# Order of TensorE's work in the first edge stage of a two-layer graph network: src transposes ahead of the centring

## The chip, the cores and the metric

One core of one Trainium2 chip. The number that counts is the device time of one execution in microseconds (us), as the median of several runs.

## The reference

`x` has 100,000 rows of 128 float32; `src` and `dst` are 25,000 edges, sorted by `dst`.

```python
# layer 0, on each edge: messages from both ends, maximum over the edges of a destination
x_col = x[col]                       # col = dst, row = src
feat = concatenate([x_col, x[row] - x_col])
messages = relu(feat @ W1 + b1) @ W2 + b2
out0 = segment_max(messages, col)    # 0 for rows without edges
x = layernorm(x + out0)
# layer 1: sum over the edges, two products, a residual product
h = x + segment_sum(x[src], dst)
x = layernorm(x + (relu(h @ W1 + b1) @ W2 + b2) + (x @ Wres + bres))
```

Most rows have no incoming edge. For them both layers are row-wise.

## The kernel before

All rows go through a dense pipeline as if they had no edges, in units of 512 rows (196 units). The rows that are destinations are computed in three edge stages and scattered over the dense result. Edges are cut into 49 groups of 512 (GROUPS), four tiles of 128 each. `walk` writes the order of the work out, and each engine follows it: a head of dense units, a stage that finds places in the table, **the first edge stage** (`step_a`), some dense units, the second edge stage (`step_b`), and dense units to the end. There is no planner; each engine has one fixed order, and semaphores hold it back.

In the first edge stage step s of TensorE works on several groups at once. psE[0] to psE[3] are four banks of PSUM:

- second product of group s-1 (`edge_product2`, L1248), ehT into psE[2];
- first product of group s (`edge_product1`, L1240 and L1242), from the transposed src rows xsT and the transposed dst rows xdT, into psE[0];
- a quarter of a dense unit (h = s mod 4: h=0 the first dense product L1137, h=1 the dense transposes L1118, h=2 and h=3 half of the second dense products L1125 and L1126);
- transposes of the finished rows x1e of group s-2 into psE[1];
- centring of group s-1 (`center_z`, L1257): four pairs of matmuls of zT with a centring matrix into psE[3];
- transposes of the rows gathered for group s+1 (`transpose_in`): the src rows (in edge_rows) into psE[0], then the dst rows (xd_early or src_bc) into psE[1].

All transposes are issued at L1118, in the helper `transpose4`, and show as one line; the operand tells them apart. A float32 matmul shows as two records.

VectorE (`step_a` there) takes per step: a reciprocal of the roots (L738), the scaling of psE[3] into x1e (L748), the running maximum along the edges (L758), the residual that makes zT (L769), statistics of the src rows (L603, L731), the copy of psE[0] into xsT for group s+1 (`copy_xs`, L718), and a dense piece.

ScalarE takes per step:

```python
def step_a(s, n, h):
    scale_xs(s)          # L1036
    relu0(s)             # L1015: psE[0] -> ehT, counts ehT_done
    copy_x1eT(s - 2)     # L1045: psE[1] -> x1eT, counts x1eT_done
    z_var(s - 1)         # L949: squares of psE[3], waits for the centring
    both_roots(s + 1)    # L1025
    copy_xd(s + 1)       # L1004: psE[1] -> xdT, counts xdT_done
    ...                  # then a dense piece by h
```

GpSimd gathers all src rows before this stage's later dst rows, and `gather_dst(g)` waits for the dst transposes of group g-7. SyncE stores x1e, its transpose and the scaled rows of each group; after the stage GpSimd gathers from that table, for which it waits until all of it is stored.

Of the kernel before, what the change touches and what calls it, by code (L numbers as in the profile page):

```python
# [23 lines left out]
def gnn_program(nc, x, src, dst, e_w1, e_b1, e_w2, e_b2, w1, b1, w2, b2, wres, bres, out):  # L24
# [29 lines left out]
    with ctx:  # L54
# [198 lines left out]
        def is_group(g):  # L253
            return 0 <= g < GROUPS

        def src_number(g):
            return TILES * (g + (SLOTS if g >= EARLY else 0))

        def dst_number(g):
            return TILES * (g + (EARLY if g < SLOTS else GROUPS))  # L260
# [7 lines left out]
        def await_landing(eng, n):  # L268

            eng.wait_ge(landed[n % FLIGHT], 16 * (n // FLIGHT + 1))  # L270

        def wait(eng, s, n):

            if n > 0:
                eng.wait_ge(s, n)
# [4 lines left out]
        def cut(t):  # L280
            return slice(t * P, (t + 1) * P)

        def xd_rows(g):

            return (src_bc if g // SLOTS % 2 else xd_early)[:, g % SLOTS, :]

        def group_rows(g):
            return edge_rows[:, g * ROWS:(g + 1) * ROWS]
# [822 lines left out]
        def _(pe):  # L1111
            t_ = nc.tensor

            def transpose4(to, rows, done=None, number=None):
                for t in range(TILES):
                    if number is not None:
                        await_landing(pe, number + t)
                    last = t_.transpose(to[:, cut(t)], rows[:, cut(t)], ident[:, :])  # L1118
                if done is not None:
                    last.then_inc(done, 1)  # L1120
# [12 lines left out]
            def first_product(n):  # L1133
                if is_unit(n):
                    pe.wait_ge(xT_done, n + 1)
                    wait(pe, hT_done, n)
                    t_.matmul(psH[:, :], wc1[:, :], xT[:, n % SLOTS, :], start=True, stop=True).then_inc(w1_done, 1)  # L1137

            def transposed(n):
                if is_unit(n):  # L1140
                    pe.wait_ge(x1_done, n + 1)
                    wait(pe, xT_done, n)
                    transpose4(psT, x1[:, n % 2, :], t_done)
# [7 lines left out]
            def second_half(n, half):  # L1151

                if half == 0:
                    pe.wait_ge(hT_done, n + 1)
                    wait(pe, o_done, n - 1)
                    product_tiles(psY[n % 2], hT[:, n % 2, :], xT[:, n % SLOTS, :], range(TILES // 2))
                else:
                    product_tiles(psY[n % 2], hT[:, n % 2, :], xT[:, n % SLOTS, :],
                                  range(TILES // 2, TILES)).then_inc(y_done, 1)
# [59 lines left out]
                second_product(n - 2)  # L1219
                place(s - 2)  # L1220

            def transpose_in(g):
                if is_group(g):
                    wait(pe, ehT_done, g)
                    transpose4(psE[0], group_rows(g), ts_done, src_number(g))
                    wait(pe, xdT_done, g)
                    wait(pe, x1eT_done, g - 2)
                    transpose4(psE[1], xd_rows(g), tx_done, dst_number(g))

            def lead_a():  # L1230
                pe.wait_ge(match_done, GROUPS)
                pe.wait_ge(places_done, GROUPS)
                transpose_in(0)

            def edge_product1(g):

                if is_group(g):
                    q = g % 2
                    pe.wait_ge(xsT_done, g + 1)
                    t_.matmul(psE[0][:, :], raw[:, W1B, :], xsT[:, q, :], start=True, stop=False)  # L1240
                    pe.wait_ge(xdT_done, g + 1)
                    t_.matmul(psE[0][:, :], wd[:, :], xdT[:, q, :], start=False, stop=True).then_inc(eh_done, 1)  # L1242

            def edge_product2(g):
                if is_group(g):
                    pe.wait_ge(ehT_done, g + 1)
                    wait(pe, max_done, g)
                    t_.matmul(psE[2][:, :], raw[:, EW2, :], ehT[:, g % 2, :], start=True, stop=True).then_inc(m_done, 1)  # L1248

            def center_z(g):  # L1250

                if is_group(g):
                    q = g % 2
                    pe.wait_ge(zT_done, g + 1)
                    wait(pe, x1e_done, g)
                    for t in range(TILES):
                        last = t_.matmul(psE[3][:, cut(t)], zT[:, q, cut(t)], center[:, :], start=t == 0,  # L1257
                                         stop=t == TILES - 1, skip_group_check=True)
                    last.then_inc(bt_done, 1)

            def transpose_x1e(g):
                if is_group(g):
                    pe.wait_ge(x1e_done, g + 1)
                    pe.wait_ge(xdT_done, min(g + 3, GROUPS))
                    wait(pe, x1eT_done, g)
                    transpose4(psE[1], x1e_rows[:, g % 2, :], xt_done)

            def step_a(s, n, h):
                edge_product2(s - 1)
                edge_product1(s)  # L1270
                if n is not None:
                    if h == 0:
                        first_product(n - 1)
                    if h == 1:
                        transposed(n)
                    if h >= 2:
                        second_half(n - 2, h - 2)
                transpose_x1e(s - 2)
                center_z(s - 1)
                transpose_in(s + 1)  # L1280


            def transpose_src(g):
# [41 lines left out]
            t_.matmul(psE[3][:, 0:P], wtmp[:, 1, :], center[:, :], start=True, stop=True)  # L1325
            t_.matmul(psE[3][:, P:2 * P], wtmp[:, 2, :], center[:, :], start=True, stop=True).then_inc(s_pe, 1)
            walk(head, dense, lead_s, step_s, lead_a, step_a, lead_b, step_b)


# [20 lines left out]
```

## Time and profile before

| what | value |
|---|---|
| median of three runs | 1114.36 us (1113.69 to 1115.48) |
| the profiled execution's own time | 1113.68 us |
| its span in the trace | 1111.9 us |
| TensorE busy | 1068.9 us, 96% |
| VectorE busy | 934.9 us, 84% |
| ScalarE busy | 896.9 us, 81% |
| GpSimd busy | 765.8 us, 69% |
| first edge stage | about 264 to 562 us of the span |
| granted TensorE clock, mean | 0.995 |

The busy shares are means over stages with different orders of work. A matmul's record overlaps the next one's, so the distance between starts is what a group of them takes, not the sum of their lengths.

### The profile page before, as it was taken

The page shows a single profiled execution, that of the slowest core. Times are in us where ns is not written, and L with a number is a line of the kernel's source. Part 1 is how long each engine was busy: PE and PEld are TensorE (multiplying, and loading weights), DVE is VectorE, ACT ScalarE, POOL GpSimd, SP SyncE. Part 2 cuts the span into 40 slices and gives each one's busy share as a digit, 9 for nine tenths or more (in the row PEclk, how much of TensorE's full clock was granted, in tenths as well). Part 3 has the DMA queues.
Part 4 walks back from the last instruction along what each step waited for, and adds up shares of the span by engine and source line. Part 5 has one row for each costly group of instructions (what it writes and reads, how often), then busy time and mean ns, then how long its engine had stood idle before and what let it go on. Part 6 is the DMA issues. An engine that isn't in the chain of part 4 may idle for free.

```text
span 1111.9 us, 27074 instructions
## 1 busy us (share of the span) xinstructions
PE 1068.9 (96%) x7463; PEld 835.6 (75%) x7463; DVE 934.9 (84%) x3645; ACT 896.9 (81%) x3888; POOL 765.8 (69%) x798
## 2 busy tenths in 40 slices
PE   5899999999999999999899999999999999999995
PEld 3677877777666666666578888888888878888884
DVE  7799888897888888888868787878787789999993
ACT  2887878787888888888897888888888887777774
POOL 6777777777777777772047777777777777777712
PEclk9999999999999999999999999999999999999998
DMA  5788877875888888877576667676756566666652
GB/s 151 214 244 247 230 244 231 246 233 152 220 222 232 248 232 221 233 223 214 164 232 198 213 191 215 190 214 191 214 166 194 172 202 217 218 217 220 218 171 86
DMA packets 172255, 231.86 MB, mean 209 GB/s; under 512 B 25658, under 2 KB 90791, under 8 KB 172106
## 3 DMA queue, kind: packets, MB, share of 16 engines
q1 hardware_dynamic: 145434, 180.66, 52.0%
q0 software_dynamic: 25088, 48.94, 17.3%
q8 instruction: 62, 1.02, 0.4%
q14 instruction: 87, 0.71, 0.2%
q10 hardware_dynamic: 1584, 0.53, 0.2%
HBM read 129.48 MB, written 102.78 MB: 209 GB/s over the span
## 4 chain that ended last, share of the span: by engine, by line
PE 65%; POOL 19%; issue 8%; DVE 4%; ACT 2%; DMA 1%; SPq 0%; POOLq 0%; DVEq 0%; ACTq 0%
POOL edge_rows L522 17%; PE psY L1125 10%; PE psY L1126 10%; PE psH L1137 10%; PE psE L1118 6%; PE psT L1118 5%; PE psE L1257 4%; PE psE L1126 4%; PE psE L1125 4%; PE psE L1293 4%; PE psE L1248 3%; PE psE L1242 3%; PE psE L1240 3%; POOL xd_early L522 1%; DVE shared L758 1%
## 5 line engine op out<-in xcount | busy, mean ns | idle before, releaser
L1125 PE MATMUL psY<-wc,hT 128*128 128x128 f32 x1568 | 304.1, 276 | 0.5 <-DVE o_rows L646 0.4
L1126 PE MATMUL psY<-wcr,xT 128*128 128x128 f32 x1568 | 303.9, 276 | 0.0
L522 POOL DMA_INDIRECT edge_rows<-x1e_table,idx x196 | 188.8, 963 | 118.5 <-issue 59.4
L526 POOL DMA_INDIRECT out<-edge_rows,idx x196 | 195.0, 995 | 100.0 <-issue 61.9
L1125 PEld LDWEIGHTS psY<-wc,hT 128*128 128x128 f32 x1568 | 240.7, 192 | 13.3 <-issue 13.3
L949 ACT ACTIVATE junk<-psY 128x128 f32<-128x128 f32 x784 | 209.3, 302 | 49.3 <-PE psY L1126 49.1
L1126 PEld LDWEIGHTS psY<-wcr,xT 128*128 128x128 f32 x1568 | 238.8, 193 | 0.0
L522 POOL DMA_INDIRECT edge_rows<-in_x,idx x196 | 189.8, 968 | 65.5 <-issue 59.4
L609 DVE TENSOR_SCALAR x<-x_in,mv,rs 128x128 f32<-128x128 f32 x784 | 221.7, 361 | 0.6
L1137 PE MATMUL psH<-xT,wc 128*128 128x512 f32 x392 | 204.5, 604 | 6.2 <-ACT xT L944 5.5
L1118 PEld LDWEIGHTS psT<-ident,x 128*128 128x128 f32 x784 | 99.2, 143 | 110.1 <-issue 104.1
L949 ACT ACTIVATION_READ_ACCUMULATOR junk<-psY 128x1 f32 x784 | 181.1, 235 | 0.0
L938 ACT ACTIVATE hT<-psH,bias_cols 128x512 f32<-128x512 f32 x196 | 137.5, 701 | 42.1 <-PE psH L1137 42.0
L603 DVE BATCH_NORM_STATS2 bn_a<-x_in 128x6 f32<-128x128 f32 x784 | 164.6, 271 | 4.4 <-DMA x_in<-in_x 4.3
L949 ACT ACTIVATE junk<-psE 128x128 f32<-128x128 f32 x392 | 102.6, 280 | 29.2 <-PE psE L1257 27.9
L1118 PE MATMUL psT<-ident,x 128*128 128x128 f32 x784 | 119.1, 275 | 5.4 <-DVE x L609 5.4
L944 ACT ACTIVATE xT<-psT 128x512 f32<-128x512 f32 x196 | 120.4, 614 | 1.9 <-PE psT L1118 1.9
L522 POOL DMA_INDIRECT xd_early<-in_x,idx x100 | 96.3, 963 | 30.5 <-issue 28.7
L522 POOL DMA_INDIRECT src_bc<-in_x,idx x96 | 93.3, 972 | 29.3 <-issue 27.7
L797 DVE TENSOR_TENSOR_SCAN shared<-mask,shared,psE 128x512 f32<-128x512 bf16 x48 | 61.4, 1280 | 54.1 <-issue 54.1
L646 DVE TENSOR_TENSOR o_rows<-psY,rs 128x512 f32<-128x512 f32 x120 | 83.0, 691 | 6.1 <-DVE rs L629 2.4
L974 ACT ACTIVATE o_rows<-psY,rs 128x128 f32<-128x128 f32 x304 | 87.4, 387 | 0.6 <-DVE rs L629 0.4
(125 smaller groups left out, 1993.4 us busy)
## 6 DMA issues: line engine op xcount, KB each, us to landing
x_in<-in_x SPq DMA_DIRECT2D x196, 256.0 KB
out<-o_rows SPq DMA_DIRECT2D x195, 256.0 KB
src_bc<-src_dram SPq DMA_DIRECT2D x49, 256.0 KB, 4.5
mask<-mask_dram SPq DMA_DIRECT2D x98, 128.0 KB
x1eT_spill<-x1eT SPq DMA_DIRECT2D x49, 256.0 KB, 2.4
x1e_table<-edge_rows SPq DMA_DIRECT2D x49, 256.0 KB, 3.5
x1e_table<-shared SPq DMA_DIRECT2D x49, 256.0 KB, 3.8
x1eT<-x1eT_spill SPq DMA_DIRECT2D x49, 256.0 KB, 3.1
```

Of the source, the lines that this page charges most:

```text
L522: nc.gpsimd.indirect_dma_start(to, None, table, bass.IndirectOffsetOnAxis(idx[:, what, t:t + 1], 0)).then_inc(landed[n % FLIGHT], 16)
L526: nc.gpsimd.indirect_dma_start(table, bass.IndirectOffsetOnAxis(idx[:, SCAT, t:t + 1], 0), frm, None, bounds_check=limit, oob_is_err=False ...
L603: last = v.bn_stats(bn[:, t, :], rows[:, cut(t)])
L609: last = v.tensor_scalar(to[:, cut(t)], rows[:, cut(t)], mv[:, t, 0:1], rs[:, t:t + 1], ALU.subtract, ALU.mult)
L938: a.activation(hT[:, n % 2, :], psH[:, :], ACT.Relu, bias=bias_cols[:, 2:3]).then_inc(hT_done, 1)
L944: a.activation(xT[:, n % SLOTS, :], psT[:, :], ACT.Copy, bias=1.0).then_inc(xT_done, 1)
L949: last = a.activation(unused[:, cut(t)], rows[:, cut(t)], ACT.Square, scale=P ** -0.5, accum_out=var[:, t, 1:2])
L974: last = a.activation(o_rows[:, n % SLOTS, cut(t)], psY[n % 2][:, cut(t)], ACT.Copy, scale=rs[:, slot, TILES + t:TILES + t + 1])
L1118: last = t_.transpose(to[:, cut(t)], rows[:, cut(t)], ident[:, :])
L1125: t_.matmul(to[:, cut(t)], h[:, cut(t)], wc2[:, :], start=t == 0, stop=False, skip_group_check=True)
L1126: last = t_.matmul(to[:, cut(t)], xt[:, cut(t)], wcr[:, :], start=False, stop=t == TILES - 1, skip_group_check=True)
L1137: t_.matmul(psH[:, :], wc1[:, :], xT[:, n % SLOTS, :], start=True, stop=True).then_inc(w1_done, 1)
```

## The change

`transpose_in` is cut in two. The src transposes of group s+1, with their waits for ehT_done and the four landings, come ahead of `center_z(s - 1)`; the dst transposes, with their waits for xdT_done, x1eT_done and their landings, stay behind it. Ahead of the stage both are called for group 0 as before. No other engine's order is touched.

```diff
--- before.py
+++ after.py
@@ -1219,10 +1219,13 @@
                 second_product(n - 2)
                 place(s - 2)
 
-            def transpose_in(g):
+            def transpose_src_in(g):
                 if is_group(g):
                     wait(pe, ehT_done, g)
                     transpose4(psE[0], group_rows(g), ts_done, src_number(g))
+
+            def transpose_dst_in(g):
+                if is_group(g):
                     wait(pe, xdT_done, g)
                     wait(pe, x1eT_done, g - 2)
                     transpose4(psE[1], xd_rows(g), tx_done, dst_number(g))
@@ -1230,7 +1233,8 @@
             def lead_a():
                 pe.wait_ge(match_done, GROUPS)
                 pe.wait_ge(places_done, GROUPS)
-                transpose_in(0)
+                transpose_src_in(0)
+                transpose_dst_in(0)
 
             def edge_product1(g):
 
@@ -1276,8 +1280,9 @@
                     if h >= 2:
                         second_half(n - 2, h - 2)
                 transpose_x1e(s - 2)
+                transpose_src_in(s + 1)
                 center_z(s - 1)
-                transpose_in(s + 1)
+                transpose_dst_in(s + 1)
 
 
             def transpose_src(g):
```

## Rows read from the trace of the kernel before

**Rows 1.** Table by window: PE, PEld, DVE, ACT, POOL busy (instructions), PEclk, DMA share, GB/s.

```profile
450.00:500.00 50.00, 48.46 (x270) 33.92 (x269) 43.66 (x139) 43.36 (x171) 38.10 (x40) 1.00 0.81 227
...
550.00:562.00 12.00, 8.26 (x44) 6.07 (x43) 6.94 (x27) 8.14 (x39) 0.00 (x0) 0.86 0.58 175
```

**Rows 2.** Instructions of the tile psE: count, min/median/max ns, first and last start.

```profile
L1257 PE MATMUL psE<-center,shared x392: 275/275/582, 273.0 to 556.5; 128*128 128x128 f32 x196
```

**Rows 3.** Timeline of TensorE, 413 to 438.5 us and the tail: start, length, [idle before, releaser].

```profile
414.27 1.16 PE L1257 MATMUL psE<-center,shared 128*128 128x128 f32 x8 [0.73 <-DVE shared L769]
415.27 0.60 PE L1118 MATMUL psE<-ident,edge_rows 128*128 128x128 f32 x4
...
417.00 1.02 PE L1240 MATMUL psE<-xsT,raw 128*128 128x512 f32 x2
417.86 1.02 PE L1242 MATMUL psE<-xdT,wd 128*128 128x512 f32 x2
...
419.61 0.60 PE L1118 MATMUL psE<-ident,shared 128*128 128x128 f32 x4
420.05 1.06 PE L1257 MATMUL psE<-center,shared 128*128 128x128 f32 x8
420.94 0.60 PE L1118 MATMUL psE<-ident,edge_rows 128*128 128x128 f32 x4
...
425.28 0.60 PE L1118 MATMUL psE<-ident,shared 128*128 128x128 f32 x4
425.91 1.16 PE L1257 MATMUL psE<-center,shared 128*128 128x128 f32 x8
...
431.65 1.08 PE L1257 MATMUL psE<-center,shared 128*128 128x128 f32 x8
...
436.45 0.60 PE L1118 MATMUL psE<-ident,shared 128*128 128x128 f32 x4
437.80 0.94 PE L1257 MATMUL psE<-center,shared 128*128 128x128 f32 x6 [0.74 <-DVE shared L769]
...
554.80 2.08 PE L1257 MATMUL psE<-center,shared 128*128 128x128 f32 x8 [1.32 <-DVE shared L769]
```

**Rows 4.** Timeline of ScalarE, 413 to 438.5 us.

```profile
415.47 0.28 ACT L949 ACTIVATE junk<-psE 128x128 f32<-128x128 f32 x1 [1.29 <-issue]
...
418.97 0.68 ACT L1015 ACTIVATE ehT<-psE,bias_cols 128x512 f32<-128x512 f32 x1
...
421.14 0.28 ACT L949 ACTIVATE junk<-psE 128x128 f32<-128x128 f32 x1 [0.30 <-PE psE L1257]
...
425.60 0.67 ACT L1015 ACTIVATE ehT<-psE,bias_cols 128x512 f32<-128x512 f32 x1
...
427.10 0.28 ACT L949 ACTIVATE junk<-psE 128x128 f32<-128x128 f32 x1 [0.36 <-PE psE L1257]
...
431.13 0.69 ACT L1015 ACTIVATE ehT<-psE,bias_cols 128x512 f32<-128x512 f32 x1
...
432.77 0.28 ACT L949 ACTIVATE junk<-psE 128x128 f32<-128x128 f32 x1 [0.32 <-PE psE L1257]
...
436.37 0.67 ACT L1015 ACTIVATE ehT<-psE,bias_cols 128x512 f32<-128x512 f32 x1
```

**Rows 5.** Timeline of VectorE, 413 to 438.5 us.

```profile
416.98 0.20 DVE L738 RECIPROCAL rs_e<-sd_e 128x8 f32<-128x8 f32 x1
...
419.13 0.75 DVE L769 SCALAR_TENSOR_TENSOR shared<-shared,bias_cols,xdT 128x512 f32<-128x512 f32 x1
...
421.58 0.69 DVE L718 COPY xsT<-psE 128x512 f32<-128x512 f32 x1 [0.50 <-PE psE L1118]
```

**Rows 6.** Timeline of ScalarE and TensorE in the stage's step 0.

```profile
267.84 0.69 ACT L1015 ACTIVATE ehT<-psE,bias_cols 128x512 f32<-128x512 f32 x1 [1.75 <-PE psE L1242]
...
268.58 0.65 PE L1118 MATMUL psE<-ident,edge_rows 128*128 128x128 f32 x4
...
269.07 0.60 PE L1118 MATMUL psE<-ident,xd_early 128*128 128x128 f32 x4
```

## The prediction

> **What bounds the kernel now.** I read the page's busy shares first, then a table by window, then the first edge stage engine by engine in order of time. The changed lines run only in that stage. In the windows, TensorE is busy 48.46 of 50 us in its middle, with the granted clock at 1.00 [rows 1]. The stage's 49 groups are centred between 273.0 and 556.5 us, eight matmuls each [rows 2]. It is periodic: one dense unit is spread over four edge steps, and the centring of the same kind of step starts at 414.27 and again at 437.80, so a cycle takes 23.53 us [rows 3]. The steps are 5.78 (h=1), 5.86 (h=2), 5.74 (h=3) and 6.15 us (h=0), from centring to centring [rows 3].
>
> What TensorE issues in a cycle, from the gaps between starts [rows 3]: a centring 0.89 when nothing stalls it (420.05, next group 420.94), four transposes 0.44 (419.61 to 420.05), a 128x512 product 0.86 (417.00 to 417.86). A step has one centring, three sets of transposes and three products: 4.79 us. The four dense pieces are a product of 0.86, four transposes of 0.44, and twice four small products of 0.89 (418.72 to 419.61). Sum: 4 x 4.79 + 3.08 = 22.2 us. So about 1.35 us of a cycle is waiting: 0.91 before the h=1 centring (transposes end issuing at 436.89, the centring starts at 437.80), 0.19 before the h=3 one (425.72 to 425.91), and 0.1 each for restarting after a stall (1.00 in place of 0.89, 414.27 to 415.27). The releaser is VectorE's L769, the residual.
>
> Two other engines are near. VectorE's idle time per step is mostly the 0.5 us before its copy of the src transposes, L718 [rows 5]. ScalarE sits idle only between the end of the edge relu (L1015) and the squares of the centred rows (L949): 1.49, 0.83, 0.95 and 1.96 us in the four steps, 5.23 per cycle. From the squares to the end of the next relu it works without a gap [rows 4]: 415.47 to 419.65 is 4.18 us, 421.14 to 426.27 is 5.13, 427.10 to 431.82 is 4.72, 432.77 to 437.04 is 4.27. Sum 18.30, and 18.30 + 5.23 = 23.53.
>
> **The change part by part.** Nothing is added or removed: the same 27,074 instructions, no DMA issue moved, no VectorE or ScalarE order changed. In each step the four src transposes (0.44 us) and their waits go from behind the centring to before it. The four landings they wait for are old: GpSimd issues all src gathers first. The dst transposes keep their place relative to the second product, still behind the centring; their two waits (xdT copied, x1eT copied) are met earlier than they come up. GpSimd's gathers wait for the dst transposes of seven groups before, which is untouched.
>
> *What it frees.* Where the centring waits for VectorE (0.91 and 0.19), src transposes fill the wait, and L718 no longer sits behind the centring. If that were all, TensorE's waits would go: 1.35 us a cycle.
>
> *What it ties.* The src transposes of group s+1 overwrite psE[0], which relu0(s) reads, so they wait for ehT_done. Behind the centring that relu was over: it ends at 419.65 and the transposes started at 420.94 [rows 3, 4]. Ahead of the centring TensorE comes to them at 420.05, 425.72, 431.65 and 436.89, and the relus end at 419.65, 426.27, 431.82 and 437.04. Three of four are late, by 0.55, 0.17 and 0.15. Queued behind the waiting transposes on TensorE is centring s-1, and ScalarE waits for that to start its squares. Behind the squares, in ScalarE's own order, stand the root, the xdT copy, the dense piece, four scalings and relu0(s+1), which releases the next step's src transposes. That is a closed ring, once per step, and it did not exist before: the centring used to depend on VectorE alone.
>
> *The ring's length.* The ScalarE part is the 18.30 us above per cycle. Its order is fixed, and none of it can move into the idle stretch but the x1eT copy (L1045, 0.6 us), which already lies there. The other part, from relu end to squares, must now be in every step: 0.05 for the semaphore, the src transposes, the centring until the squares begin. The trace has this wait once: in step 0 the src transposes are released by the relu that ends at 268.53, start at 268.58, and the next set starts at 269.07 [rows 6]. So 0.05 + 0.49. An unstalled centring at 420.05 lets the squares begin at 421.14, 1.09 later; the stalled one at 414.27 took 1.20 [rows 3, 4]. I take 1.10, since the transposes come right before it: 1.64 a step. The ring is 18.30 + 4 x 1.64 = 24.86 us. In h=2 TensorE comes 0.1 us later than the relu (its centring is issued 0.21 before the squares begin; dst transposes 0.44 and three products 2.58 bring it to 2.8 after, up to 3.0 if the last product waits for the xdT copy; with 0.89 dense and 0.44 transposes that is 4.15 to 4.35 against 4.18 + 0.05), so add 0.06: 24.92. The cycle grows by 1.39 us.
>
> Bounds of this term: with 0.44 for the transposes and 1.09, 1.58 a step and 24.62 a cycle (+1.09); with a restart of 0.11 at both, 0.05 + 0.55 + 1.20 = 1.80 and 25.50 (+1.97).
>
> *Is something slower than the ring?* VectorE: the reciprocal L738 comes 1.51 us after the squares start, the residual ends at 419.88, 2.90 us later [rows 4, 5]: ready at 4.41, while the centring needs it at 4.18 + 1.64 - 1.10 = 4.72 in the shortest step. It has 0.3 us to spare. It is busy 43.66 of 50 us [rows 1], 20.5 of 23.53 and so of 24.9. TensorE itself needs 22.2. So the ring binds.
>
> *Sum.* Centrings go in steps 1 to 49. The steps between the first and the last that still has src transposes are 46, or 11.5 cycles: 11.5 x 1.39 = 16.0 us. Step 1's centring is late by one set of transposes, 0.5. The last two steps have no src transposes and keep their time. Behind the stage everything is ordered after it: GpSimd's second gathers wait for the tables, dense units are placed by the program, so nothing absorbs the delay. Sum +16.5. Against the profiled execution's own 1113.68 us that is 1130.2; the median of the runs shown stands 0.7 higher, so 1131.
>
> On TensorE's clock, the stage's middle ran at 1.00 with waits of 0.74 in it, while in its tail, from 550 to 562, with TensorE busy 8.26 of 12 us, the mean is 0.86 [rows 1, 3]. 1.00 is the 2.4 GHz level, so part of that tail ran at 1.2. In the new cycle TensorE would be busy 22.2 of 24.9 us, about 89%, with its longest wait near 0.9, as now. I take no fall. The Trainium skill, page "TensorE: Matmul & The Clock Gate", section "HAM oscillation — how this bites in real kernels", says that TensorE waiting between bursts of matmuls drops to half clock; by it this change, which puts a wait into most steps, risks more than its ring, and that is the fourth rival below. The tail of this trace agrees that it can happen.
>
> **The rivals.**
> First, faster: the gap is filled and nothing takes its place, 1.35 x 11.5 = 15.5 us, 1098. For it: the gap and its releaser are plain in the rows, and VectorE is relieved. Against it: the relu ends after TensorE comes, in three steps of four. It would need relu ends some 0.6 us earlier. The Trainium skill, "Perfetto Trace Analysis", section "Optimization Strategy", tells one to find the gaps on the most contended engine and to make what they wait for start sooner; taken alone it argues for this rival. The rows bear out the gap, and not that the edit is free.
>
> Second, slightly faster: the src waits count once and ScalarE catches up. Waits of 0.60, 0.22 and 0.20 come in, 1.35 go: -0.33 a cycle, -4 us, 1110. Against it: ScalarE has no slack outside the stretch that the ring fills.
>
> Third, no change: the ring's stretch shrinks because squares start sooner than 1.10 after the centring, or relu ends move forward. It decides at 1.31 us per step from relu to squares (5.23 / 4), less than transposes plus the centring's issue (0.05 + 0.44 + 0.89 = 1.38), so I hold it nearly excluded.
>
> Fourth, slower still: the clock falls during the waits. A centring at the low level takes 0.9 us more (2.08 against 1.16 in the tail [rows 3]); once a cycle that adds 10 us, 1141.
>
> **How the numbers follow.** Ring: 0.83. Gap filled: 0.04. Small gain: 0.05. No change: 0.03. Clock: 0.05. The point is the ring's 1131. Its own range is +12.5 to +22.5 about the sum's bounds (11.5 x 1.09 and 11.5 x 1.97), 1126.5 to 1137.5; I open it to 1124 to 1138, since TensorE's other waits may move too. Within 0.2% (2.2 us) is about what a measurement of this kernel can't tell from no change. Slower: 0.83 + 0.05 = 0.88; same 0.03; faster 0.09.
>
> **What would show it.** The stage's centrings: the same kind of step recurring every 24.9 us, steps of about 5.9 (before h=2), 6.8, 6.4 and 5.9. TensorE's src transposes (L1118 on edge_rows) waiting with ScalarE's ehT L1015 as releaser, some 0.2 to 0.8 us in three of four steps, and no wait of the centring for L769. VectorE's idle before L718 nearly gone, and more of it before the reciprocal L738. ScalarE's idle before its squares the same in each step, about 1.0 after the x1eT copy, never 0.3. The stages before and after unchanged in length. I would be wrong if relu0(s) ended before TensorE comes to the transposes, which shows as no wait on ehT, or if L769 still held the centring back, by which VectorE would be the bound and the cycle near 23.5 or longer for another reason.

## The result and the profile after

The changed kernel takes 1130.82 us (median of five runs, 1128.58 to 1133.58) against 1114.80 us for the kernel before in the same runs. The ratio is 1.0145, with a 95% interval of 1.0126 to 1.0163: slower by 1.3 to 1.6%. The profiled execution took 1128.58 us, with a span of 1126.8.

The window in the middle of the stage answers to the first row of [rows 1]:

```profile
450.00:500.00 50.00, 46.99 (x253) 31.04 (x253) 41.27 (x131) 40.49 (x159) 37.35 (x39) 1.00 0.83 220
```

TensorE went from 48.46 busy us in 50 to 46.99, VectorE from 43.66 to 41.27, ScalarE from 43.36 to 40.49. All three are idler: none of them is the bound by itself. The clock stays at 1.00. The centrings, at L1261 now, answer to [rows 2]:

```profile
L1261 PE MATMUL psE<-center,shared x392: 275/275/421, 272.3 to 571.4; 128*128 128x128 f32 x196
```

The stage's first and last are 299.1 us apart, 283.5 before. From centring group to centring group the 48 intervals sum to 297.90 us against 281.78: 16.1 more. From the stage's first src transposes to the first centring it is 9.08 us against 8.59, so the stage as a whole grew by 16.6. What lies outside it hardly moved: the first src transposes start at 263.25 us against 264.43 (in the other runs between 262.9 and 265.3, with the same code ahead of the stage), and from the last centring group to the end of the span there are 556.6 us, 557.1 before. So this profiled execution is only 14.9 us longer than the one before, and the medians are 16.0 apart.

TensorE's timeline of one cycle, answering to [rows 3]: start, length, and in brackets the idle time before it and its releaser.

```profile
427.22 0.60 PE L1118 MATMUL psE<-ident,edge_rows 128*128 128x128 f32 x4
427.66 1.06 PE L1261 MATMUL psE<-center,shared 128*128 128x128 f32 x8
...
432.61 0.60 PE L1118 MATMUL psE<-ident,shared 128*128 128x128 f32 x4
433.94 0.66 PE L1118 MATMUL psE<-ident,edge_rows 128*128 128x128 f32 x4 [0.73 <-ACT ehT L1015]
434.43 1.06 PE L1261 MATMUL psE<-center,shared 128*128 128x128 f32 x8
...
439.35 0.60 PE L1118 MATMUL psE<-ident,shared 128*128 128x128 f32 x4
440.31 0.66 PE L1118 MATMUL psE<-ident,edge_rows 128*128 128x128 f32 x4 [0.36 <-ACT ehT L1015]
440.80 1.06 PE L1261 MATMUL psE<-center,shared 128*128 128x128 f32 x8
...
445.30 0.60 PE L1118 MATMUL psE<-ident,shared 128*128 128x128 f32 x4
446.22 0.66 PE L1118 MATMUL psE<-ident,edge_rows 128*128 128x128 f32 x4 [0.33 <-ACT ehT L1015]
446.71 1.06 PE L1261 MATMUL psE<-center,shared 128*128 128x128 f32 x8
...
452.54 0.72 PE L1261 MATMUL psE<-center,shared 128*128 128x128 f32 x5
```

The same kind of centring starts at 427.66 and at 452.54, 24.88 us apart, 23.53 before. The steps are 6.77, 6.37, 5.91 and 5.83. The src transposes (operand edge_rows) wait three times for ScalarE's ehT, and no centring waits for L769. At 427.22, the h=2 step, they start at once, 0.44 behind the x1e transposes and 0.11 behind the relu's end at 427.11. TensorE comes last there because the second part of its first product (L1246) had itself waited for ScalarE's xdT copy: in the next h=2 step the copy ends at 449.76, the product starts at 449.81, and TensorE then issues without a pause up to the src transposes at 452.10. In this step the ring closes through the xdT copy.

ScalarE's edge relus (L1015) and the first square behind each, answering to [rows 4]:

```profile
426.43 0.68 ACT L1015 ACTIVATE ehT<-psE,bias_cols 128x512 f32<-128x512 f32 x1
...
428.75 0.28 ACT L949 ACTIVATE junk<-psE 128x128 f32<-128x128 f32 x1 [0.73 <-PE psE L1261]
...
433.22 0.67 ACT L1015 ACTIVATE ehT<-psE,bias_cols 128x512 f32<-128x512 f32 x1
...
435.52 0.28 ACT L949 ACTIVATE junk<-psE 128x128 f32<-128x128 f32 x1 [1.16 <-PE psE L1261]
...
439.56 0.70 ACT L1015 ACTIVATE ehT<-psE,bias_cols 128x512 f32<-128x512 f32 x1
...
441.89 0.28 ACT L949 ACTIVATE junk<-psE 128x128 f32<-128x128 f32 x1 [1.15 <-PE psE L1261]
...
445.50 0.67 ACT L1015 ACTIVATE ehT<-psE,bias_cols 128x512 f32<-128x512 f32 x1
...
447.81 0.28 ACT L949 ACTIVATE junk<-psE 128x128 f32<-128x128 f32 x1 [1.15 <-PE psE L1261]
```

From relu end to squares it is 427.11 to 428.75, 433.89 to 435.52, 440.26 to 441.89 and 446.17 to 447.81: 1.64, 1.63, 1.63 and 1.64 us. Before they were 1.49, 0.83, 0.95 and 1.96. From squares to the next relu's end nothing changed: 428.75 to 433.89 is 5.14, before 5.13. The stretch from relu to squares, uneven before, is now the same in each step. In three steps ScalarE sits idle for 1.15 or 1.16 us of it; in the h=2 step it is 0.73, since the x1eT copy starts later there.

VectorE, answering to [rows 5]:

```profile
428.45 0.66 DVE L718 COPY xsT<-psE 128x512 f32<-128x512 f32 x1
...
430.26 0.20 DVE L738 RECIPROCAL rs_e<-sd_e 128x8 f32<-128x8 f32 x1 [0.37 <-ACT sd_e L1025]
...
434.63 0.69 DVE L718 COPY xsT<-psE 128x512 f32<-128x512 f32 x1 [0.27 <-PE psE L1118]
...
437.03 0.20 DVE L738 RECIPROCAL rs_e<-sd_e 128x8 f32<-128x8 f32 x1 [1.60 <-ACT sd_e L1025]
```

It waits little or not at all for the transposes at L718, and up to 1.60 us for ScalarE's root at L738. Who waited for whom from 285 to 570 us: us in total, times, longest:

```profile
ACT junk L949 <- PE psE L1261: 47.3, 46, 1.2
DVE rs_e L738 <- ACT sd_e L1025: 43.0, 46, 1.6
...
PEld psE L1118 <- ACT ehT L1015: 22.7, 32, 1.1
...
PE psE L1118 <- ACT ehT L1015: 15.1, 31, 0.9
...
PE psE L1261 <- DVE shared L769: 0.9, 1, 0.9
```

One centring in this window still waits for the residual: that of group 47, which has no src transposes ahead of it.

### The profile page after: what moved, and what is told of

Same layout as the page of the kernel before. It is cut to its first block, busy times and chain, and to the rows that moved or that the text cites. A ratio compares the mean times of both kernels' runs of the same rounds, so it can differ in the third digit from the quotient of the medians.

```text
span 1126.8 us, 27074 instructions
## 1 busy us (share of the span) xinstructions
PE 1074.7 (95%) x7463; PEld 828.6 (74%) x7463; DVE 932.1 (83%) x3645; ACT 896.4 (80%) x3888; POOL 770.6 (68%) x798
## 4 chain that ended last, share of the span: by engine, by line
PE 57%; POOL 19%; ACT 13%; issue 9%; DMA 1%; DVE 1%; SPq 0%; ACTq 0%; POOLq 0%; DVEq 0%
POOL edge_rows L522 17%; PE psY L1125 10%; PE psY L1126 10%; PE psH L1137 9%; PE psE L1118 5%; ACT junk L949 5%; PE psT L1118 5%; PE psE L1125 4%; PE psE L1126 4%; PE psE L1298 4%; PE psE L1261 4%; ACT edge_rows L1036 3%; ACT ehT L1015 2%; POOL xd_early L522 1%; ACT o_rows L974 1%
```

## The experiments

The theory is a ring, a chain of waits that leads back to its own start one step later: relu0(s), src transposes, centring, squares, root, xdT copy, dense piece, scalings, relu0(s+1). The rivals were that TensorE's order costs by itself, that ScalarE is short of time wherever the work stands, and that each step with the new order costs its own share. Cycle is the distance of two centrings of the same kind of step in the middle of the stage. Each ratio is to runs of the kernel before on the same chip, whose medians lay between 1114.45 and 1115.09.

| kernel | median us | ratio to before | cycle us |
|---|---|---|---|
| before | 1114.80 | 1 | 23.53 |
| changed | 1130.82 | 1.0145 (1.0126 to 1.0163) | 24.88 |
| scale_behind_new | 1109.63 | 0.9957 (0.9943 to 0.9971) | 23.11 |
| scale_behind_old | 1114.17 | 0.9994 (0.9985 to 1.0003) | 23.53 |
| src_first_h1_only | 1114.66 | 0.9994 (0.9985 to 1.0003) | 23.5 |
| dense_piece_first | 1107.24 | 0.9930 (0.9917 to 0.9944) | 22.67 |
| dose_in_ring_new | 1151.80 | 1.0332 (1.0315 to 1.0350) | 26.93 |
| dose_in_gap_new | 1129.95 | 1.0138 (1.0121 to 1.0155) | 24.86 |
| dose_in_ring_old | 1114.99 | 1.0007 (0.9990 to 1.0024) | 23.6 |
| dense_piece_first_new | 1129.37 | 1.0135 (1.0116 to 1.0154) | 24.86 |
| dense_first_h1_src_first | 1108.41 | 0.9952 (0.9939 to 0.9966) | 22.94 |
| both_moves_old | 1108.67 | 0.9954 (0.9936 to 0.9972) | 22.85 |

**ScalarE's scalings behind the relu, in the changed kernel.**

```diff
             def step_a(s, n, h):
-                scale_xs(s)
                 relu0(s)
+                scale_xs(s)
                 copy_x1eT(s - 2)
```

> The changed kernel, with ScalarE's four scalings of the src rows (L1036 group, 1.17 us a step) moved from ahead of relu0(s) to behind it. TensorE's order is that of the changed kernel. Ring theory (relu0(s), then src transposes, then centring, then ScalarE's squares and the rest up to relu0(s+1)): 1.17 us leave the ring and lie in the stretch from relu to squares, which is 1.64 us long and holds only the x1eT copy of 0.6. Relu0 then comes right behind the first product, the src wait on ehT falls to 0.1 or less, and the cycle of four steps goes from 24.88 to about 23.0 us: 1108 (1103 to 1113). Rival (the order itself is what costs: the centring stands 0.44 us later in each step, and everything behind it follows, whoever releases the transposes): no change, 1131, and the ehT wait stays or turns into another wait of the same length.

1109.63 us, 21 us under the changed kernel with TensorE's order unchanged. The order itself does not cost. By the ring's own sum, 24.88 less four times 1.17 is 20.2 us, below TensorE's own work of 22.2, so the ring should no longer bind. TensorE's timeline here:

```profile
429.74 0.60 PE L1118 MATMUL psE<-ident,shared 128*128 128x128 f32 x4
430.18 0.60 PE L1118 MATMUL psE<-ident,edge_rows 128*128 128x128 f32 x4
430.62 1.06 PE L1261 MATMUL psE<-center,shared 128*128 128x128 f32 x8
...
435.11 0.60 PE L1118 MATMUL psE<-ident,shared 128*128 128x128 f32 x4
435.62 0.66 PE L1118 MATMUL psE<-ident,edge_rows 128*128 128x128 f32 x4
436.18 1.16 PE L1261 MATMUL psE<-center,shared 128*128 128x128 f32 x8
...
447.94 1.06 PE L1261 MATMUL psE<-center,shared 128*128 128x128 f32 x8
```

At 430.18 the src transposes start 0.44 behind the x1e ones, with no wait. At 435.62, the h=1 step with its short dense piece, they start 0.51 behind, so the wait is 0.07. The cycle is 23.11 (424.83 to 447.94). With the relu earlier, this order of TensorE is 0.4% faster than before. What holds the cycle 0.9 us above TensorE's own work is not shown by a run.

**The same move in the kernel before.** The same diff, on the old order.

> The kernel before, with the same move of the four scalings behind relu0(s). TensorE's order is that of before. Ring theory: there is no ring to shorten, the cycle is set by VectorE's residual ahead of the centring and by TensorE's own work, so 1114.5 (1112 to 1117). Rival (relu0 is late in general and any kernel gains from having it earlier): as many us gained as in the changed kernel, about 1098.

1114.17 us, no change. The gain of 21 us is there only where the src transposes stand ahead of the centring. In the old order an early relu is worth nothing. The two runs differ in TensorE's order alone, and there the new order is the faster one: 0.9957 (0.9943 to 0.9971) against 0.9994 (0.9985 to 1.0003).

**Work added on ScalarE, inside and beside the ring.** `extra` is a tile of its own.

```diff
                 both_roots(s + 1)
                 copy_xd(s + 1)
                 if n is not None:
+                    a.activation(extra[:, :], raw[:, 0:TILES, :].rearrange("p n d -> p (n d)"), ACT.Copy, bias=1.0)
                     if h == 0:
                 ...
```

In dose_in_gap_new the same line, under the same condition, stands between `copy_x1eT(s - 2)` and `z_var(s - 1)`.

> The changed kernel, with one more ScalarE copy of 128x512 (0.5 to 0.6 us) in each of the stage's 48 steps with a dense piece, behind the xdT copy. It adds work and changes no result. Ring theory: it lies in the ring and is paid in full, 47 times 0.5 to 0.6: +23 to +28 us, about 1156. Rival (the ring does not bind, TensorE's or VectorE's own order does): ScalarE has 4.2 us of idle time a cycle, room for four copies, so well under half of it, 1131 to 1140.

> The changed kernel, with the same extra copy in the same steps, between the x1eT copy and the squares. Ring theory: that stretch lies beside the ring's other branch (src transposes and centring, 1.64 us against 0.6 for the x1eT copy and 0.55 for the extra one), so it costs nothing: 1131 (1129 to 1135). Rival (ScalarE is short of time as such): +23 us or a large part of it.

> The kernel before, with the extra copy behind the xdT copy in the same steps. Ring theory: no ring in this order, but ScalarE has only some 0.3 us to spare in two steps of a cycle, so squares and xdT copy come up to 0.45 us late there and the second part of the first product with them: 0 to 0.5 us a cycle, 1117 (1114 to 1121). Rival (each added 0.5 us on ScalarE is paid wherever): +23 us, 1138.

ScalarE's timeline in dose_in_ring_new, the xdT copy, the extra copy and what follows:

```profile
430.45 0.57 ACT L1005 COPY xdT<-psE 128x512 f32<-128x512 f32 x1
430.92 0.63 ACT L1059 ACTIVATE extra<-raw 128x512 f32<-128x512 f32 x1
431.45 0.68 ACT L939 ACTIVATE hT<-psH,bias_cols 128x512 f32<-128x512 f32 x1
```

The extra copy takes 0.53 us from start to start. In the ring of the changed kernel the cycle grows from 24.88 to 26.93, 0.51 a step, all of it paid; from first to last centring group the stage grows by 23.1 us. The profiled executions lie 23.2 us apart (1128.58 and 1151.75). The median rose by 21.0, and by 21.9 against dose_in_gap_new on the same chip. That is less than the +23 to +28, about 1156, that I expected, and far above the rival's 1131 to 1140. Part of it may be that the changed kernel's runs spread over 5 us; the trace has the copy at 0.51 us a step. Beside the ring, in the same kernel and in the same steps, it costs nothing (24.86). In the old order it costs next to nothing (23.6 against 23.53, and 1.0007 with an interval of 0.9990 to 1.0024). So ScalarE's time is not short; its place in the ring is what counts.

**VectorE's dense piece ahead of its copy of the src transposes.**

```diff
             def step_a(s, n, h):
                 ...
                 xs_var(s)
-                copy_xs(s + 1)
                 if n is not None:
                     ...
+                copy_xs(s + 1)
```

> The kernel before, TensorE's order untouched; on VectorE the dense piece of a step goes ahead of the copy of the src transposes (L718), where VectorE sat idle for 0.5 us a step. Ring theory has the same reading of the kernel before as the prediction: the wait of 0.91 us before the h=1 centring belongs to VectorE's round (copy, dense piece, reciprocal, scaling, scan, residual, centring, transposes, copy). With the dense piece in the idle stretch the round shortens by 0.5 us in h=0 and by some 0.3 in h=2: cycle about 22.8, 1106 (1102 to 1111). Rival (TensorE would be late by the first product then, since the copy comes later, or the residual is not what sets the pace): no gain, 1114.

> The changed kernel, with VectorE's dense piece ahead of the copy of the src transposes, the move that took 7.7 us from the kernel before. Ring theory: VectorE is not in the ring and waits for ScalarE's root in every step, so the move gains nothing here: 1130.5 (1128 to 1133). Rival (the new order's loss and VectorE's round are separate costs that add up): about 1123.

In the old order 0.7% is gained, 7.8 us against the runs of before on the same chip. VectorE's timeline, in a step with h=0:

```profile
428.59 0.87 DVE L603 BATCH_NORM_STATS2 bn_x<-edge_rows 128x6 f32<-128x128 f32 x4
429.50 0.38 DVE L731 BATCH_NORM_AGGREGATE mv_e<-bn_x 128x2 f32<-128x6 f32 x4
429.79 1.08 DVE L609 TENSOR_SCALAR x<-x_in,mv,rs 128x128 f32<-128x128 f32 x4
430.79 0.68 DVE L718 COPY xsT<-psE 128x512 f32<-128x512 f32 x1
431.44 0.20 DVE L738 RECIPROCAL rs_e<-sd_e 128x8 f32<-128x8 f32 x1
```

No idle time is left between statistics, dense piece, copy and reciprocal, where 0.5 us were lost before, and the cycle is 22.67, 0.43 above TensorE's own 22.24 us (4 x 4.79 + 3.08).

The median gains less than the cycle promises: 12 cycles of 0.86 us would be 10.3. The stage of this trace is only 6.2 us shorter (275.60 against 281.78 from first to last centring), because one step early in it takes 9.10 us in place of 5.58. TensorE waits there for gathered dst rows to land:

```profile
291.99 0.33 PE L1118 MATMUL psE<-ident,src_bc 128*128 128x128 f32 x1 [0.86 <-DMA src_bc<-in_x,idx]
293.20 0.33 PE L1118 MATMUL psE<-ident,src_bc 128*128 128x128 f32 x1 [0.88 <-DMA src_bc<-in_x,idx]
293.37 1.81 PE L1248 MATMUL psE<-ehT,raw 128*128 128x512 f32 x2
294.97 1.91 PE L1240 MATMUL psE<-xsT,raw 128*128 128x512 f32 x2
```

and the row of the table by window for 294 to 296 us:

```profile
294.00:296.00 2.00, 2.00 (x4) 0.84 (x3) 0.72 (x1) 1.90 (x6) 1.46 (x2) 0.50 0.90 248
```

The granted clock was 0.50 there, the 1.2 GHz level, and the two products took 1.60 and 1.71 us from start to start in place of 0.86. Waits of this kind stand at the same place in most runs, 0.48 us in the kernel before and up to 1.13 in dense_first_h1_src_first, where the clock stayed at 1.00. So the cycle in the middle, and not the median, tells what a move does to the chain of work.

In the changed order the same move gives a cycle of 24.86 and a ratio of 1.0135, by whose interval it can't be told from the changed kernel. VectorE set the pace before and does not after. They are not two costs that add up.

**Src transposes first in one step of four.**

```diff
-                transpose_src_in(s + 1)
+                if s % A_STEPS == 1:
+                    transpose_src_in(s + 1)
                 center_z(s - 1)
+                if not (s % A_STEPS == 1):
+                    transpose_src_in(s + 1)
                 transpose_dst_in(s + 1)
```

> The changed kernel, but the src transposes go ahead of the centring only in steps with h=1 (one of four), where the kernel before left TensorE idle for 0.91 us; in the other three they stand behind it as before. Ring theory: a step whose neighbours are not tied has nothing to build up on, ScalarE is not held in every step, the transposes fill the idle time in one step, and about 0.4 us a cycle are gained: 1109 (1105 to 1114). Rival (each step with the new order costs its own share, a quarter of the loss of 16 us): 1118.

1114.66 us: both expectations were wrong. There is neither a quarter of the loss nor the gain I expected from filling the idle time. Against the rival this run is weak evidence: the h=1 step is the one that had 0.91 us of idle time to absorb a cost, and none of the other three was run alone. That the closed ring costs, and not each step, rests on the runs above. TensorE's timeline around that step:

```profile
437.75 0.60 PE L1118 MATMUL psE<-ident,shared 128*128 128x128 f32 x4
438.39 0.66 PE L1118 MATMUL psE<-ident,edge_rows 128*128 128x128 f32 x4
439.11 1.16 PE L1261 MATMUL psE<-center,shared 128*128 128x128 f32 x8
...
444.16 0.60 PE L1118 MATMUL psE<-ident,shared 128*128 128x128 f32 x4
444.83 1.16 PE L1261 MATMUL psE<-center,shared 128*128 128x128 f32 x8
```

and VectorE's residuals and the reciprocal between them:

```profile
438.28 0.78 DVE L769 SCALAR_TENSOR_TENSOR shared<-shared,bias_cols,xdT 128x512 f32<-128x512 f32 x1
...
441.81 0.20 DVE L738 RECIPROCAL rs_e<-sd_e 128x8 f32<-128x8 f32 x1 [0.70 <-ACT sd_e L1025]
...
444.03 0.75 DVE L769 SCALAR_TENSOR_TENSOR shared<-shared,bias_cols,xdT 128x512 f32<-128x512 f32 x1
```

The src transposes do fill the wait. The centring still starts at 439.11, 0.05 behind the residual's end (438.28 + 0.78). TensorE is then 0.44 ahead, and loses it at the next centring, which waits until the next residual has ended (444.03 + 0.75). That one could not be earlier: centring at 439.11, squares, root, reciprocal at 441.81 after 0.70 of idle time behind ScalarE's root, scaling, scan, residual, centring at 444.83. It is a second ring, 5.6 to 5.7 us long, through ScalarE and VectorE, that exists in both orders. The prediction has its length (1.10 us from centring to squares, 4.41 from there to the residual's end, 0.05 to the centring: 5.56), but held it only against the new ring, and not against the gap that was to be filled. The steps shown are 6.16, 5.72, 5.96 and 5.74 us where they were 6.15, 5.78, 5.86 and 5.74. The second is 5.66, or 0.01 less, in most other cycles: 0.12 won behind the h=1 centring, and 0.10 lost behind the next, which now starts behind a stall. This second ring is read from the trace; no run here changed its length alone.

**Two combinations,** tried for a version faster than both.

> Src transposes ahead of the centring in h=1 steps alone, together with VectorE's dense piece ahead of its copy. In dense_piece_first the h=1 centring waits 0.17 us and restarts for 0.11, and nothing else waits for the residual. If the src transposes could use that idle time, at most 0.28 us a cycle: 1104. But in src_first_h1_only the time filled in was given back at the next centring, since from one centring to the next at least 5.56 to 5.66 us pass through squares, root, reciprocal, scaling, scan and residual. By that chain the gain is nil and the relu, which ends late in this step, may cost a little: 1107 (1105 to 1110).

> The kernel before with both moves, ScalarE's scalings behind relu0 and VectorE's dense piece ahead of the copy. TensorE issues 22.2 us of work a cycle and dense_piece_first stands at 22.67, so at most 0.45 us a cycle are left, 5 us. The scalings move did nothing by itself in the old order: 1107 (1104 to 1109). If relu0 or the x1eT copy held anything in dense_piece_first, up to 3 us less.

Neither beats dense_piece_first. Its h=1 step, from the centring of h=0 to that of h=1, takes 5.58 us, where TensorE has only 4.79 + 0.44 = 5.23 of work; the other three take 5.64 to 5.77 and are filled by TensorE's own work and one restart. So by these rows what is left above 22.24 us lies for the most part in the second ring. With the src transposes first in h=1, that centring comes 5.98 instead of 5.58 us after the one before, since 0.44 us of transposes now stand ahead of it where little was left to fill; the next comes after 5.56 instead of 5.78, which gives back 0.22 of it and is the length of the second ring behind a centring that was not stalled; the one after that comes 0.11 later (5.78 instead of 5.67), since it starts behind a stall. With both moves the scalings stand ahead of the x1eT copy, which the dst transposes wait for: in the h=1 step of the trace the copy ends at 437.48 and they start at 437.58, 0.58 behind the src transposes instead of 0.44, and the relu itself is no longer waited for by anyone. The fastest version measured, by its median and by its cycle, is the old order with dense_piece_first's move, 1107.24 us, 0.9930 (0.9917 to 0.9944).

## Why the prediction was right

The forecast was 1131 us, the measured median 1130.82. The mechanism is the one that the runs show. That the two numbers agree to 0.2 us is luck: the changed kernel's five runs spread over 5 us, and the median of before was 1114.36 us where the forecast started from and 1114.80 in the runs of the result. Point by point:

- **The ring binds.** Shown: it disappears when the scalings leave it (1109.63), takes 0.51 us a step when 0.53 are put into it, takes nothing when they are put beside it, and is indifferent to a VectorE gain that the old order turns into 0.7%. In the h=2 step TensorE comes last and the ring closes through the xdT copy, which the prediction had as a possibility.
- **Its length.** Forecast were 18.30 us a cycle on ScalarE and 1.64 a step from relu to squares; measured are 18.34 and 1.63 to 1.64. Cycle 24.92 forecast, 24.88 found. The h=2 step's case, where TensorE comes last, is also there: no wait for ehT before 427.22. The 0.06 us added for it did not show: 0.06 more until the transposes start, but 0.44 for them in place of 0.49, so the stretch is 1.64 there too. The 5.23 us a cycle in which the prediction has ScalarE idle hold its four x1eT copies of 0.6 as well; the sum uses the whole stretch, so it is not touched.
- **The sum.** 16.5 us were forecast against before, 16.0 for 46 steps and 0.5 ahead of the first centring. In the trace the 46 steps grew by 16.2 us, the way to the first centring by 0.5, and the last two steps took 0.1 less: 16.6. The median grew by 16.0.
- **Nothing absorbs it behind the stage.** 556.6 us from the last centring group to the end, 557.1 before.
- **The step that was too generous** is the one on what the change frees. I wrote that if nothing were tied, TensorE's waits of 1.35 us a cycle would go (they are 1.29, 23.53 less 22.24). src_first_h1_only had 0.44 us of it to win and won next to nothing, because the second ring stands at 5.6 to 5.7 us. It did not touch the forecast, since the first ring is longer in all steps. But the first rival's 1098 asked for too much: its condition, relus that end before TensorE comes, is all but met in scale_behind_new, and the time there is 1109.63. The rule of the Trainium skill that stood beside it ("Perfetto Trace Analysis", section "Optimization Strategy": find the gaps on the engine and make what they wait for start sooner) served dense_piece_first well, where the awaited residual really did come sooner, by 0.86 us a cycle. The changed kernel did not make the residual sooner; it put other work into the gap.
- **The second rival** (waits counted once, -4 us) failed as expected: 0.60, 0.22 and 0.20 us of late relus became 0.89, 0.52 and 0.48, each from the point at which TensorE has issued the x1e transposes (433.05, 439.79 and 445.74) to the start of the src transposes. They grew since the relu is late by what it delayed itself one step earlier.
- **The clock.** The changed kernel's stage ran at a granted clock of 1.00 from 264 to 550 us, with TensorE waiting in three steps of four, 0.9 us at the longest. The fall of which the Trainium skill warns ("TensorE: Matmul & The Clock Gate", section "HAM oscillation — how this bites in real kernels") did not come with these waits. It can come in this stage: in dense_piece_first the clock was at 0.50 behind two waits of 0.86 and 0.88 us with one transpose between them.

## What to carry to other kernels

Filling an engine's idle time with a later instruction is free only if that instruction's own waits are over by then. Otherwise all that stands behind it in the queue inherits its wait, and if the awaited engine waits for one of these in turn, a ring closes: add up its pieces once round and compare with the period. A dose on one engine, once inside and once beside the suspected ring, tells whether it binds. Ahead of filling a gap, ask what lets the awaited result come sooner; here one VectorE move beat every order of TensorE that was run.

## What I had not expected of the hardware

The fall of the clock in dense_piece_first, above, was one thing: with waits of similar length in dense_first_h1_src_first (0.44 and 1.13 us) it did not come, and no run shows what decides it. Otherwise little. The wait in the ring was more exact than I had bounded it: 1.63 to 1.64 us against bounds of 1.58 to 1.80, step after step, and the hand-over from relu end to transpose start was 0.05 us each time (433.89 to 433.94, 440.26 to 440.31, 446.17 to 446.22). A 128x512 copy on ScalarE that shows as 0.63 us cost 0.53 in the queue, so doses have to be reckoned from start to start.
